# Input statistics a slot later in layers 0 and 1, and a regrouped mixing: scalings by image, other waits for loads and zeros, constants loaded in one block

## The reference

```python
x = x + L0(_gn(x))   # shift every image by (dy, dx), integers from its mean features
x = x + L1(_gn(x))   # 3x3 convolution of sign(x) with signed weights summed over 4 sets
x = x + L2(_gn(x))   # spectral layer
x = x + L3(_gn(x))   # spectral layer, other weights
# spectral layer:
v  = einsum('kn,bcxn->bcxk', D, x)                 # cosine transform of one axis
v  = rfft(v, axis=-2)[..., :32, :32]               # Fourier transform of the other, 32x32 modes kept
vt = einsum('ijab,ejab->eiab', R, v)               # mixing: 32x32 channels, one matrix per mode, complex
u  = irfft(...);  u = einsum('kn,bcxk->bcxn', D, u)
out = relu(u + x @ W.T + b)
```

## Time and profile before

| | us |
|---|---|
| three runs, median (lowest to highest) | 3744.3 (3741.0 to 3749.56) |
| profiled execution, its own time | 3783.59 |
| its span | 3781.8 |
| PE busy | 3024.4 (80%) |
| DVE busy | 2752.2 (73%) |
| ACT busy | 1478.2 (39%) |
| POOL busy | 36.9 (1%) |

### The profile page before, as it was taken

How to read it: one execution, slowest core, us unless ns; L and a number is a source line. 1 busy time by engine, 2 the same in 40 slices (tenths; PEclk the granted TensorE clock), 3 DMA queues, 4 the chain that set the end, 5 groups by cost and what they waited for, 6 DMA issues and landing times. The chain is left out here.

```text
span 3781.8 us, 58575 instructions
## 1 busy us (share of the span) xinstructions
PE 3024.4 (80%) x17264; PEld 1393.2 (37%) x17264; DVE 2752.2 (73%) x3864; ACT 1478.2 (39%) x2708; POOL 36.9 (1%) x23
## 2 busy tenths in 40 slices
PE   0288888888888888889937888989898835999997
PEld 0033334333334333344425333333333315444443
DVE  3887777787778687788342767676767644899998
ACT  3466666576666566664423322222222213000000
POOL 0000000000000000000010000000000010000000
PEclk9988888798888798889966999999898866999998
DMA  4676665666656566665274564646465353999998
GB/s 145 184 224 191 200 188 179 192 203 194 191 181 195 173 200 196 204 195 172 91 137 184 230 252 183 248 179 252 188 244 203 139 124 102 342 394 385 379 384 306
DMA packets 272195, 808.65 MB, mean 214 GB/s; under 512 B 85466, under 2 KB 119774, under 8 KB 261108
## 3 DMA queue, kind: packets, MB, share of 16 engines
q1 hardware_dynamic: 212948, 488.15, 40.9%
q10 hardware_dynamic: 58368, 316.72, 21.6%
q0 software_dynamic: 608, 0.63, 0.1%
HBM read 479.39 MB, written 329.56 MB: 214 GB/s over the span
## 5 line engine op out<-in xcount | busy, mean ns | idle before, releaser
L1397 ACT ACTIVATE B_junk<-B_im,B_nk 128x896 bf16<-128x896 f32 x224 | 232.7, 1039 | 749.3 <-DVE B_im L1455 610.4
L839 DVE SCALAR_TENSOR_TENSOR A_image<-A_cps,A_cbias,A_image 128x896 f32<-128x896 f32 x224 | 257.4, 1149 | 239.5 <-PE A_cps L470 239.1
L509 PE MATMUL A_vps<-A_tout,a_k_dctj 112*32 112x512 f32 x896 | 294.6, 792 | 150.6 <-ACT A_tout L614 150.6
L470 PE MATMUL A_cps<-A_sign,A_cfull 128*128 128x448 bf16 x1344 | 404.7, 384 | 7.7 <-issue 7.7
L1648 PE MATMUL C_ring<-C_im,C_wnorm 128*128 128x448 f32 x896 | 388.1, 572 | 23.7 <-DVE C_ubuf L1705 18.3
L1315 PE MATMUL B_ring<-B_rout,iB_k_rowf 128*64 128x512 f32 x896 | 306.6, 774 | 118.4 <-DVE B_rout L1448 118.4
L1343 PE MATMUL B_ring<-B_im,B_wnorm 128*128 128x448 f32 x896 | 384.9, 571 | 7.1 <-DVE B_wnorm L1426 4.9
L1455 DVE SCALAR_TENSOR_TENSOR B_im<-B_ring,B_im 128x896 f32<-128x896 f32 x224 | 239.0, 1084 | 183.9 <-PE B_ring L1353 182.3
L475 PE MATMUL A_cps<-A_sign,A_cedge 32*32 32x448 bf16 x1344 | 363.7, 379 | 0.0
L477 PE MATMUL A_cps<-A_sign,A_cedge 32*32 32x448 bf16 x1344 | 363.4, 378 | 0.0
L614 ACT ACTIVATE A_tout<-A_aps 112x512 f32<-112x512 f32 x448 | 246.1, 589 | 288.8 <-PE A_aps L498 288.3
(11 more groups left out here) (193 smaller groups left out, 3444.6 us busy)
## 6 DMA issues: line engine op xcount, KB each, us to landing
A_rin<-in_x SPq DMA_DIRECT2D x2016, 112.0 KB, 2.4
x2s<-A_image ACTq DMA_DIRECT2D x112, 896.0 KB, 4.6
B_im<-x2s SPq DMA_DIRECT2D x112, 896.0 KB, 9.7
x3s<-B_im ACTq DMA_DIRECT2D x112, 896.0 KB
C_im<-x3s SPq DMA_DIRECT2D x112, 896.0 KB, 11.9
out<-C_rout ACTq DMA_DIRECT2D x192, 256.0 KB
out<-C_rout ACTq DMA_DIRECT2D x192, 192.0 KB
out<-C_rout ACTq DMA_DIRECT2D x64, 128.0 KB
```

The lines of the kernel that those rows point to most:

```text
L470: return nc.tensor.matmul(banks[:, s, 0:LPN], cfull[:, tap, :], lines(n, s, slice(0, P), 0, tap), start=(tap == 0), stop=(tap == 2), skip_ ...
L509: last = nc.tensor.matmul(vps[32 * g:32 * g + 32, :], con["k_dctj"][:, half, :], tout[G % OUTS][:, half, :], start=(half == 0), stop=(half ...
```

## The change

It has three parts. **(1)** In layers 0 and 1, ACT does the input statistics of the x tiles of slot s-1 in slot s, the square right behind the sum; in slot 14 `lower` stands behind `square`; and DVE works out the guess itself, from the first 56 values per partition of tile 0. **(2)** In the mixing, the scaling goes by image: DVE scales 11 images and ACT 5, two instructions each of 64x512, all of them before the first product; PE and ACT's copies wait once for all; SP holds the weights of chunks 1 to 3 until the spectra have landed; POOL starts its zeros at once, in eight pieces. **(3)** The constants of a mixing and of the layer behind it are loaded in one block ahead of the mixing, so that there is one block and one barrier less for each of the two.

```diff
-        def x_ops(k):
-            return [("sum", k)] + [("square", j) for j in {15: (13, 14, 15)}.get(k, (k - 2,)) if j >= 0]
+        def stat_tiles(s):
+            return x_tiles(s - 1) if s else range(0)
...
             def x_tile(b, q, k, tile):
                 sum_x(b, q, k, tile)
-                if k >= 2:
-                    square_x(b, q, k - 2)
-                if k == TILES - 1:
-                    square_x(b, q, k - 1)
-                    square_x(b, q, k)
+                square_x(b, q, k)
...
+                    if has_v and 1 <= s <= UNITS:
+                        square(b, q, s - 1)
                     if has_x and s == 14:
                         lower(b + 1, (q + 2) % 3)
-                    if has_v and 1 <= s <= UNITS:
-                        square(b, q, s - 1)
                     if has_v and s in (5, 9, 13):
                         copy_rows(b, (s - 5) // 4)
-                    for k in x_tiles(s) if has_x else ():
+                    for k in stat_tiles(s) if has_x else ():
                         x_tile(b + 2, (q + 2) % 3, k, tile_no(b, x_at(k)))
...
-            def guess(b):
-                dve.wait_ge(junk_done, junk_x(b, ("sum", 0)) + 1)
-                nc.vector.tensor_scalar(nx[:], xsum[:, 0:1], -1.0 / TN, None, ALU.mult).then_inc(nx_ready, 1)
+            def guess(b, q):
+                dve.wait_ge(tile_turned, 1 if isinstance(b, int) and b == 0 else tile_no(b - 2, x_at(0)) + 1)
+                link(nc.vector.tensor_reduce(sm[:, 30:31], image[q][:, 0:2 * CHQ], AX.X, ALU.add))
+                nc.vector.tensor_scalar(nx[:], sm[:, 30:31], -0.5 / CHQ, None, ALU.mult).then_inc(nx_ready, 1)
...
-                        if k == 2:
-                            guess(b + 2)
...
                         turn_x(far, k, x_at(k) % RING, tile_loaded(b, x_at(k)))
+                        if k == 0:
+                            guess(b + 2, far)
...
-        raw_in = sem("raw_in")
+        raw_in = [sem(f"raw_in{i}") for i in range(4)]
+        act_scaled = sem("act_scaled")
...
+        by_scalar = range(2, NB, 3)
+        def scale(engine, b):
+            for high in range(2):
+                rows = slice(64 * high, 64 * high + 64)
+                last = engine(moving[rows, :, high * NB + b], raw[rows, b, :], gscale[rows, b:b + 1])
+            return last
...
             sp.dma_start(bcol[:], bb[:, None]).then_inc(small_in, 16)
+            for g in range(4):
+                sp.wait_ge(raw_in[g], 16 * NB // 4)
             for k in range(1, CHUNKS):
...
-            pool.wait_ge(mean_in, 3)
-            nc.gpsimd.memset(moving[0:64, :, NB:2 * NB], 0.0)
-            nc.gpsimd.memset(moving[64:128, :, 0:NB], 0.0).then_inc(zeroed, 1)
+            for i in range(4):
+                cols = slice(i * BANK // 4, (i + 1) * BANK // 4)
+                nc.gpsimd.memset(moving[0:64, cols, NB:2 * NB], 0.0)
+                last = nc.gpsimd.memset(moving[64:128, cols, 0:NB], 0.0)
+            last.then_inc(zeroed, 1)
...
             for k in range(CHUNKS):
-                pe.wait_ge(scaled, k + 1)
+                if k == 0:
+                    pe.wait_ge(scaled, 1)
...
-            for k in range(WB):
+            act.wait_ge(mean_in, 3)
+            for n, b in enumerate(by_scalar):
+                if n == 2:
+                    same_rows(0)
+                act.wait_ge(raw_in[4 * b // NB], 16 * NB // 4)
+                scale(by_act, b).then_inc(act_scaled, 1)
+            for k in range(1, WB):
                 same_rows(k)
             for n in range(CHUNKS * CH):
                 act.wait_ge(prod_full, n + 1)
                 if n == 0:
-                    act.wait_ge(scaled, CHUNKS)
+                    act.wait_ge(scaled, 1)
...
             neg_rows(0)
-            dve.wait_ge(raw_in, 16 * NB)
-            for k in range(CHUNKS):
-                for high in range(2):
-                    rows = slice(64 * high, 64 * high + 64)
-                    link(nc.vector.tensor_tensor(moving[rows, CM * k:CM * (k + 1), high * NB:(high + 1) * NB],
-                                                 raw[rows, :, CM * k:CM * (k + 1)].rearrange("p b m -> p m b"),
-                                                 gscale[rows, :].unsqueeze(1).to_broadcast([64, CM, NB]), ALU.mult))
-                if k == 0:
-                    link(nc.vector.scalar_tensor_tensor(out=moving[0:32, 0, 0:NB], ...))
-                dve.sem_inc(scaled, 1)
-                if k + 1 < CHUNKS:
-                    neg_rows(k + 1) if k + 1 < WB else None
+            for b in range(NB):
+                if b not in by_scalar:
+                    dve.wait_ge(raw_in[4 * b // NB], 16 * NB // 4)
+                    last = scale(by_dve, b)
+            link(last)
+            dve.wait_ge(act_scaled, len(by_scalar))
+            link(nc.vector.scalar_tensor_tensor(out=moving[0:32, 0, 0:NB], ...))
+            dve.sem_inc(scaled, 1)
+            for k in range(1, WB):
+                neg_rows(k)
...
-            phase("m" + tag, ["k_pair"], lambda con: mix_modes(...))
-            phase("i" + tag, ["k_invs", "k_dcti"] + ([] if last else ["k_rowf", "k_colf"]), lambda con: last_layer(...) if last else third_layer(...))
+            phase(tag.lower(), ["k_pair", "k_invs", "k_dcti"] + ([] if last else ["k_rowf", "k_colf"]),
+                  lambda con: mixed_layer(con, layer, tag, src, dst, last))
```

More of the change, by code:

```diff
@@ L288, in junk_place @@
                     place["y", s - 1] = len(place)
-                for k in x_tiles(s) if has_x else ():
-                    for op in x_ops(k):
-                        place[op] = len(place)
+                for k in stat_tiles(s) if has_x else ():
+                    for op in ("sum", "square"):
+                        place[op, k] = len(place)
             return place
@@ L885, in _ @@
                 turn_x(0, k, k % RING, 64 * (k // RING + 1))
-                if k == 2:
-                    guess(0)
+                if k == 0:
+                    guess(0, 0)
             for i in (0, 1, 2, 4, 3):
@@ L932, in _ @@
             body(0, 0, None, True, True, True, False)
-            PER = 41
+            PER = 42
             start = at["n"]
@@ L1073, in same_rows, with by_act @@
                 last.then_inc(w_same, 1)
-            for k in range(WB):
+            def by_act(dst, src, factor):
+                return nc.scalar.activation(dst, src, ACT.Copy, scale=factor)
+            act.wait_ge(mean_in, 3)
[5 more added lines that the diff above has]
+            for k in range(1, WB):
                 same_rows(k)
@@ L1777, in phase, with mixed_layer @@
                 run(con)
+        def mixed_layer(con, layer, tag, src, dst, last):
+            mix_modes(nc, NB, ins[layer + "R_real"], ins[layer + "R_imag"], ins[layer + "W"], ins[layer + "b"], con, statm, gscale,
+                      spec, mixed, tag)
+            if last:
+                last_layer(nc, NB, tag, ins[layer + "W"], con, gscale, mixed, src, dst)
+            else:
+                third_layer(nc, NB, tag, ins[layer + "W"], con, gscale, mixed, src, dst, statm, spec)
         phase("a_", ["k_fwdr", "k_dctj", "k_ident", "k_pair", "k_same", "k_rows", "k_cols"],
@@ L1782, in program @@
         for layer, tag, src, dst, last in (("L2_conv_", "B_", x2s, x3s, False), ("L3_conv_", "C_", x3s, out, True)):
-            phase("m" + tag, ["k_pair"],
-                  lambda con: mix_modes(nc, NB, ins[layer + "R_real"], ins[layer + "R_imag"], ins[layer + "W"],
-                                        ins[layer + "b"], con, statm, gscale, spec, mixed, tag))
-            phase("i" + tag, ["k_invs", "k_dcti"] + ([] if last else ["k_rowf", "k_colf"]),
-                  lambda con: last_layer(nc, NB, tag, ins[layer + "W"], con, gscale, mixed, src, dst) if last else
-                  third_layer(nc, NB, tag, ins[layer + "W"], con, gscale, mixed, src, dst, statm, spec))
+            phase(tag.lower(), ["k_pair", "k_invs", "k_dcti"] + ([] if last else ["k_rowf", "k_colf"]),
+                  lambda con: mixed_layer(con, layer, tag, src, dst, last))
 _INS = ["x", "L0_conv_W", "L0_conv_b", "L1_conv_W", "L1_conv_b", "L2_conv_R_real", "L2_conv_R_imag", "L2_conv_W",
```

10 lines of the change are left out of this document (6 added, 4 removed).

## The result

The changed kernel takes 3809.5 us in the median of four runs (3789.4 to 3826.9), the kernel before beside it 3746.8 (3741.0 to 3749.6): a ratio of 1.0133, with a 95% interval of 1.0074 to 1.0192. It is slower; 3717.5 was forecast, with a range up to 3741. Run again beside the experiments (`e12`, twelve runs) the same text gave 1.0073 (1.0044 to 1.0102).

A forecast was written before the change was run, and what follows sets the result against it. No engine alone was taken as the bound, but a ring of waits among DVE, PE and ACT. Mixing -26.3, constants -4.3 and part 1 +4 gave -26.6 us, from 3744.3 to 3717.5; own range 3700 to 3732, whole range 3688 to 3741.

The forecast's parts named there:

- the term of part 1 that prices the half clock: Layers 0 and 1, before convolution 12: longer PE idle might make half clock the rule, 13 us; a third taken, +4 us.
- no gain in slots 5 to 14: Layers 0 and 1: ACT's and PE's shorter waits gain nothing there, since DVE's chain goes on and PE then waits for DVE.
- the +4 of the sum: Layers 0 and 1: the whole cost forecast for the later statistics, +4 us, between -22 and +25.
- Part 1 makes it slower: Rival, chance 0.09: long waits before convolutions in three slots an image, each 2.64 us dearer, +103 at most; slower from +38, 3752.
- the ring's waits were on the path: Rival, chance 0.20: PE's 139 us of waits for `A_tout` are partly gain; 3668 at a third, 3702 at a tenth.
- `lower` and the guess: Layers 0 and 1: both cost nothing, covered by DVE's waits for PE; uncovered, the guess would be 7 us.
- The border's 2.48 us: Image border: DVE's wait for a square goes, but DVE waits for PE instead; without that cover it would be 25 us.
- Part 2: Mixing: scaling by image before the first product starts item 4 earlier, -12.4 us in the first and -13.9 in the second.
- the strided scaling: Mixing: each of DVE's 22 scalings takes 0.50 us, bounds 0.40 and 1.0; a rival at 1.0, chance 0.17, gives about 3738.
- ACT's bound: Mixing: item 4 also waits for ACT's `same_rows(2)` and first copy, until 1972.1 in the first and 3130.45 in the second.
- The hold on the second and third weights: Mixing: holding chunks 1 and 2 until the spectra land opens no gap; up to 2 us would cost some +3 together.
- Part 3: Constants: 4.24 and 3.31 us go behind the mixings, +2.1 and +1.1 are added ahead; net -2.1 and -2.2.

The follow-up runs named there:

- e12: The changed kernel again, word for word, twelve runs beside the kernel before: 3792.1 us, ratio 1.0073 (1.0044 to 1.0102).
- e10: The changed kernel plus 24 matmuls for nothing an image on PE, before the slot 11 average that waits for DVE: 3749.9 us, ratio 0.9979 to the kernel before.
- e2: The kernel before with only the changed mixing and constants, layers 0 and 1 as before: 3747.8 us, ratio 0.9919 to the kernel before.
- e3: The kernel before with only the guess on DVE and `lower` behind `square`, statistics and mixing as before: 3760.8 us, ratio 0.9983.
- e7: The changed kernel with the mixing's scalings written contiguously instead of every 128 bytes, output wrong: 0.50 us a scaling on DVE, one run of 3772.0 us.
- e4: The changed kernel with PE's two input-statistics averages moved from the ends of slots 11 and 12 to behind convolutions 12 and 13: 3750.0 us, ratio 0.9967.
- e1: The kernel before with only layers 0 and 1 as changed, mixing and constants old: 3853.0 us, ratio 1.0196 to the kernel before.

## Why the prediction was wrong

**The step that failed** is the term of part 1 that prices the half clock: "If this makes the half clock the rule, it costs 5.81 - 4.84 = 0.97 us an image, 13 us in 13 images", of which a third went into the sum. Its direction was right, and so was the gap in front of convolution 12, 5 us forecast and 66.8 / 12 = 5.6 measured; so was "no gain in slots 5 to 14" (no wait of DVE at adds 5 to 11 in either trace). Even inside the distance for which it was worked out it held: 5.47 us in the mean, +0.63 an image. Wrong was to count the half clock only there, in the distance in which I had found it. It went on through convolution 13 and across the border, and from there to add 4 PE is what DVE waits for. DVE's waits for the convolution over twelve images rose from 13.4 to 16.6 us an image: 0.6 at add 12, 0.7 at add 13, 0.8, 0.4, 0.7 and 0.3 at adds 0 to 3, less 0.3 at add 4. The period rose from 112.6 to 116.6 us (the 118 us that was put to an image ahead of the result was too long from the start). Three profiles with the old order end layers 0 and 1 at 1913.2, 1922.8 and 1916.6, five with the delay and without added work at 1972.9, 1990.8, 1982.0, 1959.7 and 1964.7: 1974.0 - 1917.5 = 56.5 us against the +4 of the sum. Taking "a third" of 13 was a choice without a row; with all of 13 it would have been wrong too.

**The row that could have told it** was there in the trace of before: PE's wait for `A_tout` ahead of convolution 12, 3.92 us in the mean of twelve images, stood in front of L509, the column transform, and its eight matmuls took 3.63 us (the earlier trace rows has one such wait, 4.04, and the 3.63) where they take 1.91 at full clock (at 1892.52 in the changed kernel's trace). DVE does not wait for that product, so the recovery was paid by work with room to spare. I had read the wait as harmless idle time and not as the place where the clock was lost and won back.

**The rival that came true** was "Part 1 makes it slower", at 0.09: and it had the cause right, the clock, but not the place: it put a long wait in front of the convolutions of up to three slots, each 2.64 us dearer. Measured is one such wait an image, and a clock that stays low over six adds behind it, each 0.3 to 0.8 us later. That the sum is 3.95 us an image, one and a half times 2.64, is luck. Its threshold was also added up wrongly: one and a half slots are 2.64 x 1.5 x 13 = 51 us, and the +38 stands for 1.1 slots. The runs e10 and e12 show the mechanism: with the same order, more work for nothing in the gap gives a higher clock and a shorter kernel. The rival that the ring's waits were on the path finds no support: in e10 PE's waits for `A_tout` are down to 15.5 us over twelve images and the clock is up, and yet the kernel (0.9979, with some 4 us an image of added matmuls in it) is not faster than e2 with the old order (0.9919). Its two times were also 1 to 2 us off their own terms, which give 3667.4 and 3699.8. What it had not seen is that the waits do not go: the 129.6 us for `A_tout` are found again as 66.8 and 62.9 us in the two new places.

**`lower` and the guess** cost nothing (e3), as forecast. The border's 2.48 us went and gave nothing: DVE waited for PE in their place, and more.

**Part 2** was right in mechanism. Item 4 starts 60.49 us after the first weights' issue instead of 69.82, and 60.48 instead of 71.07: -9.3 and -10.6 against -12.4 and -13.9. The term that was mis-sized is the strided scaling, 0.73 us for the 0.50 that I took: 22 x 0.23 = 5.1 us later in each; in the second, 1.1 of it was covered, since ACT's bound had been the later one there. In the first mixing 2.2 came back, since the first four items took 14.8 us with the wait behind them instead of 16.93. The Trainium skill's penalty for an access that goes to a new line ("SBUF — State Buffer", section "Door 1: The DMA port swizzle") is borne out so far as that writes 128 bytes apart cost 0.23 us more than contiguous ones (e7); whether the lines are the reason no run tells. At 0.73 us the instruction was a little nearer to my 0.50 than to the upper bound of 1.0. The hold on the second and third weights cost 0.9 us (third chunk 48.7 us after the first issue, 47.8 before), and ACT was not the bound. **Part 3** came out as worked out ahead of the mixing (+2.2 and +1.1), and behind it gave 3.3 and 3.0 us instead of 4.2 and 3.3: -3.0 instead of -4.3. Parts 2 and 3 together: -23.0 instead of -30.6.

**What stays open.** What puts the third layer at 995 or 1023 us in one execution or the other was not tried. Nor is it told apart by a run how much of e4's gain is the earlier convolution and how much the clock. The delay costs 46 us in one execution and 78 in another (layers 0 and 1 end at 1959.7 in e7, at 1990.8 in e1, at 1913.2 before). That goes with the granted clock between adds 11 and 13, 0.60 and 0.83 in e7 and 0.53 and 0.61 in e1, but no run shows what sets it.

## What to carry to other kernels

When an edit takes away a wait of the matrix engine that is off the critical path, ask what runs at half clock behind it now, and what will run behind the place to which the idle time moves: an idle gap is cheapest in front of work that nobody waits for. Follow the granted clock from the gap up to the place where the engine sets the pace, not only to the next wait. If the gap can't be moved, a few matmuls for nothing in it are worth trying: 24 of them made up for 0.9% here. They only brought the kernel back to where it had been, though; leaving the edit out (e2, 0.9919) looks better still. And compare medians of several runs before you read a cause from one profile: three of the profiles here are the luckiest of their kernel.

## What the runs showed of the hardware

- Work for nothing on PE made the kernel faster: ratios 1.0073 (1.0044 to 1.0102) and 0.9979 (0.9944 to 1.0014) for 0 and 24 matmuls of 128x384 an image, with 1.0026 for 12 between them and clear of neither.
- The same matmuls with the same idle time in other places got another clock: 17.0 and 16.9 us of PE idle an image, 0.83 and 0.80 granted, 95.6 and 99.7 us busy.
- 512 float32 written 128 bytes apart take 0.73 us on VectorE and 1.17 on ScalarE, next to each other 0.50 and 0.73.
- The third layer, the same text each time, took 990 to 998 us in ten profiles and 1022 to 1024 in four.
